# Layer 1's projections from one product of weights, q and k parts stored one by one, and four scatters or gathers under way

## The reference

```python
# layer 0
h = layernorm(x) * (1 + ca) + sa
q, k, v = split(h @ w_qkv.T)                # 16 heads of 8
x = x + ga * (softmax(q k' * SCALE) v @ w_out.T + b_out)
h = layernorm(x) * (1 + cb) + sb
comb = the two largest of softmax(h @ gate_w.T), of 8 experts, elsewhere 0
x = x + gb * (sum over e of comb[:, e] * swiglu_e(h) + swiglu_shared(h))   # hidden 352 and 192
# layer 1
q, k, v = h @ wq_lat @ wq_heads, h @ wk_lat @ wk_heads, h @ wv_lat @ wv_heads   # latents of 32
x = x + ga * (softmax(causal(q k' * SCALE)) v @ w_proj + b_proj)
x = x + gb * sum over e of comb[:, e] * (relu(h @ W1[e])**2 @ W2[e])            # 8 experts of 128
ga, gb = (2 * (g >= 0) - 1) * max(|g|, 0.25)     # in both layers
```

## Time and profile before

| | |
|---|---|
| Time, three runs | 1190.44, 1190.77, 1201.79 us; median 1190.77 |
| The profiled execution | 1188.06 us, its span 1185.7 us |
| PE busy | 1053.7 us, 89% of the span |
| DVE, ACT, POOL busy | 891.5, 743.6, 410.2 us |
| Mean granted clock of PE | 0.948 of full speed |

### The profile page before, as it was taken

How to read it: one execution, slowest core, us unless ns; L and a number is a source line. 1 busy time by engine, 2 the same in 40 slices (tenths; PEclk the granted TensorE clock), 3 DMA queues, 4 the chain that set the end, 5 groups by cost and what they waited for, 6 DMA issues and landing times.

```text
span 1185.7 us, 22774 instructions
## 1 busy us (share of the span) xinstructions
PE 1053.7 (89%) x8372; PEld 539.5 (45%) x8372; DVE 891.5 (75%) x1809; ACT 743.6 (63%) x1235; POOL 410.2 (35%) x462
## 2 busy tenths in 40 slices
PE   4588988889899997899999998998998999999985
PEld 2121222215354454455556565656664344444454
DVE  5899888988788876796667876787666777778354
ACT  3157777677566665667665665456665676866853
POOL 2100222252123434532244424343125663333452
PEclk9569999989999999999999999998999799999998
DMA  3815253656738558448577485675733533521110
GB/s 104 188 32 128 75 135 109 185 157 170 208 96 264 185 158 225 137 132 231 169 203 223 144 255 164 179 222 160 190 116 107 113 109 83 140 62 34 57 38 18
DMA packets 114798, 169.21 MB, mean 143 GB/s; under 512 B 19248, under 2 KB 79024, under 8 KB 114688
## 3 DMA queue, kind: packets, MB, share of 16 engines
q1 hardware_dynamic: 109376, 156.49, 46.3%
q0 software_dynamic: 4736, 10.49, 3.1%
q10 hardware_dynamic: 576, 0.79, 0.2%
HBM read 109.07 MB, written 58.62 MB: 141 GB/s over the span
## 4 chain that ended last, share of the span: by engine, by line
PE 39%; DMA 21%; DVE 18%; issue 9%; ACT 6%; POOL 4%; SPq 1%; POOLq 0%; ACTq 0%; DVEq 0%
DMA gr<-d_y,pos 10%; DVE nm L873 9%; PE ps L698 9%; PE ps L681 4%; PE ps L660 4%; PE ps L759 4%; DMA d_h<-hx,pos 3%; PE ps L775 3%; PE ps L782 3%; PE ps L767 3%; ACT ES L1221 3%; DMA DR<-d_r 2%; DMA d_u<-US 2%; DMA d_m<-nmp 2%; ACT xn L1153 1%
## 5 line engine op out<-in xcount | busy, mean ns | idle before, releaser
L873 DVE TENSOR_REDUCE nm<-ps 128x2 f32<-128x1024 f32 (+3 forms) x512 | 508.3, 1016 | 89.7 <-PE ps L666 56.3
L1221 ACT ACTIVATE ES<-ps 128x1024 f32<-128x1024 f32 (+3 forms) x512 | 431.3, 863 | 178.5 <-PE ps L681 93.4
L698 PE MATMUL ps<-ES,VS 128*9 128x512 f32 (+3 forms) x2048 | 236.1, 539 | 0.8 <-DVE hdx L1057 0.5
L660 PE MATMUL ps<-KS,QS 48*128 48x512 bf16 (+3 forms) x1024 | 187.3, 365 | 39.7 <-DVE nm L873 28.8
L681 PE MATMUL ps<-QS,KS 51*128 51x512 bf16 (+3 forms) x1024 | 181.7, 354 | 24.5 <-DVE nm L873 12.9
L759 PE MATMUL ps<-hsT,wst 128*128 128x128 f32 x1104 | 152.5, 284 | 3.9 <-DVE nm L873 1.2
L759 PEld LDWEIGHTS ps<-hsT,wst 128*128 128x128 f32 x1104 | 135.6, 193 | 33.6 <-issue 29.5
L681 PEld LDWEIGHTS ps<-QS,KS 51*128 51x128 bf16 x1024 | 50.2, 94 | 190.4 <-issue 73.5
L660 PEld LDWEIGHTS ps<-KS,QS 48*128 48x128 bf16 x1024 | 50.5, 95 | 170.0 <-DVE nm L873 67.7
L1423 POOL TENSOR_TENSOR ya<-ya,yS 128x512 f32<-128x512 f32 x49 | 62.7, 1279 | 154.3 <-DVE yS L1117 154.2
L1403 POOL DMA_INDIRECT gr<-d_y,pos x64 | 66.7, 1042 | 108.4 <-DMA gr<-d_y,pos 65.8
(11 more groups left out here) (187 smaller groups left out, 1341.2 us busy)
## 6 DMA issues: line engine op xcount, KB each, us to landing
wst<-we SPq DMA_DIRECT2D x92, 576.0 KB, 5.0
d_u<-US SPq DMA_DIRECT2D x64, 256.0 KB
KS<-d_k SPq DMA_DIRECT2D x64, 192.0 KB, 5.3
...
d_q<-sp SPq DMA_DIRECT2D x16, 384.0 KB, 2.8
d_k<-sp SPq DMA_DIRECT2D x16, 384.0 KB, 2.6
...
```

The lines of the kernel that those rows point to most:

```text
L660: mm = eng.matmul(psum[:, bank[u][a], 0:n], QS[m][r:r + KA, pr, 128 * t:128 * t + 128], KS[m][r:r + KA, pr, 0:n], start=True, stop=i < NB)
L698: mm = eng.matmul(psum[32 * a:32 * a + 9, b, q0:S], VS[i % 3][:, j, 4 * g + a, :], ES[(2 * (NT * (NG * i + g) + j) + a // 2) % NES][:, a % ...
L873: eng.tensor_reduce(nm[f][:, :].rearrange("p (a c) -> p a c", a=2)[:, :, 4 * pr + t], ps2("score", i, f, pr, t)[:, :, 0:n], AX.X, ALU.max, ...
L1221: eng.activation(ES[(2 * n + pp) % NES][:, :, 0:S - q0], ps2("bscore", i, f, g, j, pp)[:, :, 0:S - q0], ACT.Exp, scale=SC1 if i >= NB else ...
```

## The change

1. **Latents.** `p_lat` and `p_latc` go. Once, PE multiplies the latents by the head weights (`w_mm`, 384 columns), ACT copies the product over the head weights (`w_cp`), and in layer 1 q, k and v come from hP directly. The host lays the latents out transposed; the product is made on the chip.
2. **Parts of q and k.** Each part is a step of its own on SP and is issued when that part is ready. sr has two buffers, one for q and one for k. The four loads of a stack go KS, QS, KS, QS with the halves taken crosswise.
3. **Ones.** One memset makes rows of ones in a weight buffer not yet used (`c_one`, 32x1024), and eight DMAs carry three rows each into KS. `bscore` waits for them all, and so does the first use of that weight buffer.
4. **Scatters and gathers.** Each waits for the one four before it, not two; the scatters' semaphores are regrouped to four.
5. **Gates.** `m_fin` has five operations in place of nine, on two of three column groups at a time.
6. **The planner's numbers** are set anew, which moves steps on all engines.

The diff, cut to its core:

```diff
-SHIFT = {"t": -0.12, "s": 1.02, ... "d": 1.41, "x": 1.14, ... "g": -0.96, ...}
+SHIFT = {"t": -0.11, "s": 1.11, ... "d": 1.34, "x": 1.09, ... "g": -0.9, ...}
...
-    MOVES = {"stack": 2.7, "p_store": 3.4, ...
+    MOVES = {"stack": 3.8, "p_store": 0.8, ...
...
-SPREAD = 2.6, 1.8
+SPREAD = 2.4, 2.1
...
+        add("DVE", ("c_one",), 1.2, -1.0, [("m_one", 0)])
     for m in range(NSTK):
-        add("DVE", ("c_ks", m), 2.3, -1.0 + 0.3 * m, [("p_sub", 0, 1) if m else ("p_stats", 0)])
+        add("SP", ("c_ks", m), 0.8, 0.1 + 0.1 * m, [("c_one",)], lag=2.5)
...
+    add("PE", ("w_mm",), 0.75, 6.5, [("ld", "w1")], opens=1)
+    add("ACT", ("w_cp",), 0.4, 6.5, [("w_mm",)], closes=[("w_mm",)])
...
-                    add("DVE", ("g_w", i0, t), 0.58, u, [two, last, ("g_x", i0 - 1), ("m_st", 1)])
+                    add("DVE", ("g_w", i0, t), 0.75, u, sent[-2:] + [("g_x", i0 - 1), ("m_st", 1)])
...
-                elif k == "p_lat":
-                    i = u[1]
+                elif k == "w_mm":
+
                     q.wait_ge(*on("ld", "w1"))
-                    q.wait_ge(*on("p_ht", i))
-                    open_banks(u)
-                    eng.matmul(ps(*u), w1s[:, W1["lat"]:W1["lat"] + 128], hP, start=True, stop=True).then_inc(s[k], 1)
+                    open_banks(u)
+                    eng.matmul(ps(*u)[:, 0:384], w1s[:, W1["lat"]:W1["lat"] + 128], w1s[:, W1["q"]:W1["q"] + 384],
+                               start=True, stop=True).then_inc(s[k], 1)
...
-                elif k == "p_latc":
-                    i = u[1]
-                    q.wait_ge(*on("p_lat", i))
...
-                    eng.activation(lat, ps("p_lat", i), ACT.Copy).then_inc(s[k], 1)
+                elif k == "w_cp":
+                    q.wait_ge(*on("w_mm"))
+                    eng.activation(w1s[:, W1["q"]:W1["q"] + 384], ps("w_mm")[:, 0:384], ACT.Copy).then_inc(s[k], 1)
...
-                    if n:
-                        q.wait_ge(s["g_ga", 2 * ((n - 1) % 4) + c], 16 * ((n - 1) // 4 + 1))
+                    if n >= 2:
+                        q.wait_ge(s["g_ga", 2 * ((n - 2) % 4) + c], 16 * ((n - 2) // 4 + 1))
...
+                elif k == "c_ks":
+                    q.wait_ge(*on("c_one"))
+                    for a in range(2):
+                        eng.dma_start(KS[u[1]][64 * a + KA:64 * a + KB, :, :].rearrange("k h t -> k (h t)"),
+                                      ones[0:KB - KA, :].bitcast(BF16)).then_inc(s["ld", k], 16)
                 elif k == "p_store":
-                    i, n = u[1:]
-                    q.wait_ge(*on("p_hi", i, n))
-                    q.wait_ge(*on("p_mid", i, n))
-                    q.wait_ge(*on("p_lo", i, n))
-                    to = (d_q, d_k)[n][i]
-                    for c, (r, step, reps) in enumerate(PLACES[n]):
-                        eng.dma_start(bass.AP(tensor=to.tensor, offset=to.offset + r * 128 * S, ap=[[S, 128], [step * 128 * S, reps], [1, S]]),
-                                      sp[n][:, c:c + 1, :].broadcast_to([128, reps, S])).then_inc(s["p_store", n], 16)
+                    i, n, c = u[1:]
+                    q.wait_ge(*on(("p_hi", "p_mid", "p_lo")[c], i, n))
+                    to, (r, step, reps) = (d_q, d_k)[n][i], PLACES[n][c]
+                    eng.dma_start(bass.AP(tensor=to.tensor, offset=to.offset + r * 128 * S, ap=[[S, 128], [step * 128 * S, reps], [1, S]]),
+                                  sp[n][:, c:c + 1, :].broadcast_to([128, reps, S])).then_inc(s["p_store", n], 16)
...
-                    for a in range(2):
-                        for to, of in ((KS, d_k[i]), (QS, d_q[i])):
+                    for h in range(2):
+                        for a, to, of in ((h, KS, d_k[i]), (1 - h, QS, d_q[i])):
```

More of the change, by code:

```diff
@@ L243, in plan @@
         for n in range(2):
             u = i + 0.05 + 0.05 * n
-            add("PE", ("p_proj", i, n), 0.95, u, [x, ("ld", f"w{l}"), ("p_store", i - 1, n), ("p_sub", i - 1 + n, 1 - n)], opens=1)
-            add("ACT", ("p_hi", i, n), 0.49, u, [("p_proj", i, n), ("p_store", i - 1, n)])
-            add("DVE", ("p_sub", i, n), 0.6, u, [("p_hi", i, n), ("p_lo", i - 1 + n, 1 - n)], closes=[("p_proj", i, n)])
+            add("PE", ("p_proj", i, n), 0.95, u, [x] + ready, opens=1)
+            add("ACT", ("p_hi", i, n), 0.49, u, [("p_proj", i, n)] + [("p_store", i - 1, n, c) for c in range(3)])
@@ L254, in plan @@
             add("SP", ("stack", i, f), 2.1, i + 0.2 + 0.1 * f,
-                [("p_store", i, 0), ("p_store", i, 1), ("c_ks", (2 * i + f) % NSTK), ("bscore", i - 2, f, 1, NT - 1, 1)], lag=3.4)
+                [("p_store", i, n, c) for n in range(2) for c in range(3)] + [("bscore", i - 2, f, 1, NT - 1, 1)], lag=3.4)
         for f in range(2):
@@ L285, in plan @@
                     add("PE", ("bscore", i, f, g % 2, j, pp), 0.01 + 0.22 * n / 512 + 0.06 * (not big), u + 0.03 * pp,
-                        [("max_ld", i, f)] + exps[-2:-1] + old, mode="half", opens=2)
+                        [("max_ld", i, f)] + [("c_ks", m) for m in range(NSTK) if i == 0] + exps[-2:-1] + old, mode="half", opens=2)
                     add("ACT", ("expo", i, f, g % 2, j, pp), 0.06 + 2 * n * 0.00083, u + 0.03 * pp,
@@ L355, in plan @@
                         n = min(4, NMT - j)
-                        add("SP", ("x_ld", q, L), 0.45, u - 0.2, [two, last]
+                        add("SP", ("x_ld", q, L), 0.45, u - 0.2, sent[-4:]
                             + [("x_turn", q, L - 2) if L > 1 else ("x_turn", q - 1, NXL - 2 + L)], lag=3.1)
@@ L385, in plan @@
                     for k in range(2):
-                        add("POOL", ("g_ga", i0, t, k), 1.28, u, [("x_st", q, L) for L in range(NXL)] + [two, ("g_w",) + n2], lag=2.1)
-                        two, last = last, ("g_ga", i0, t, k)
-                    add("DVE", ("g_w", i0, t), 0.58, u, [two, last, ("g_x", i0 - 1), ("m_st", 1)])
+                        add("POOL", ("g_ga", i0, t, k), 1.28, u, [("x_st", q, L) for L in range(NXL)] + [sent[-4], ("g_w",) + n2], lag=2.1)
+                        sent.append(("g_ga", i0, t, k))
+                    add("DVE", ("g_w", i0, t), 0.75, u, sent[-2:] + [("g_x", i0 - 1), ("m_st", 1)])
                 add("POOL", ("g_x", i0), 2.6, u, [("g_w", i0, NT - 1), ("g_gc", i0), ("s_x", i0)])
@@ L543, in program @@
         for k in total:
-            if k not in DMAS and k not in ("ld", "p_store", "r_sc", "g_ga", "d_out", "c_h", "c_code"):
+            if k not in DMAS and k not in ("ld", "p_store", "r_sc", "g_ga", "d_out", "c_h", "c_code", "c_ks"):
                 s[k] = ctx.enter_context(nc.semaphore(k))
@@ L552, in program @@
             s["p_store", n] = ctx.enter_context(nc.semaphore(f"p_store{n}"))
-            for c in range(2):
-                s["r_sc", n, c] = ctx.enter_context(nc.semaphore(f"r_sc{n}{c}"))
         for name in ("t_mul", "r_hm", "rstd_a"):
@@ L557, in program @@
         rstd_a = {u: 2 * n + 1 for n, u in enumerate(u for u in todo["POOL"] if u[0] in ("p_rstd", "f_rstd"))}
+        for n in range(4):
+            s["r_sc", n] = ctx.enter_context(nc.semaphore(f"r_sc{n}"))
         for n in range(8):
@@ L1160, in _ @@
                     q.wait_ge(*on("m_one", l))
[L1161 removed]
+                    if w == 0 and i:
                         q.wait_ge(*on("p_v", i - 1))
@@ L1362, in _ @@
                         p = i // 2 - 1
-                        for c in range(2):
-                            q.wait_ge(s["r_sc", p % 2, c], 128 * (p // 2 + 1))
+                        for m in range(4):
+                            q.wait_ge(s["r_sc", m], 64 * (p + 1))
                     eng.tensor_tensor(hx[i % 2][:, :, :], xn[1][:, :, :], g[:, 2:3, :].broadcast_to([128, NT, 128]),
```

130 lines of the change are left out of this document (59 added, 71 removed).

## The result

| | |
|---|---|
| The changed kernel, four runs | 1214.12 to 1223.94 us, median 1220.55 |
| The kernel before, beside it | 1189.44 to 1201.79 us, median 1190.61 |
| Ratio | 1.0227, 95% interval 1.0163 to 1.0291: slower, by 1.6 to 2.9% |
| Forecast | 1174, range 1156 to 1192: the time lies outside, on the other side |

What follows compares the result with a forecast made beforehand. PE was taken as the bound, with DVE's row maxima setting the pace from 34 to 75 us. From 1188.06 us, -1.5 - 1.0 - 7.1 - 7.0 = -16.6 gave 1171.5, or 1174 for the median; range 1156 to 1192.

Steps and rivals of the forecast that it cites:

- The start: Loads and stores before the first score: earlier issue wins 1.5 us, between -4.8 and +2.7.
- The gates: DVE's nine operations from 75.52 to 78.53 us become five: -1 us, between 0 and -3.
- The latents: Sixteen PE records, 8.8 us, go and one product comes: -7.1 us, between 0 and -8.0.
- The gathers: DVE's combines in four pairs: four under way quicken gathers, stalls shrink to 3.2 us a pair, -7 us.
- the 1.8: The pace forecast for gathers with four under way: one each 1.8 us, beside 3.5 before.
- the moved steps: Steps that the planner's new numbers move on all engines: 0, with 5 us either way.
- The term of the scatters: Scatters ahead of the experts' tiles, where PE is at 96%: 0, to -4 us.
- The slower one: Rival: DVE comes to the combines too early and stalls longer: 1204 to 1247 us, chance 0.11.
- Gains turned into waiting: Rival: PE's saved time goes into waits for row maxima, gathers stall as before: 1188 us, chance 0.18.

Runs made afterwards that it cites:

- a4gap: The changed kernel, lists and waits of four kept, with POOL clearing 192 columns of a spare tile behind each scatter and gather: 1200.9 us, ratio 1.0085.
- p4: The changed kernel with lists written anew for two transfers under way, but waits of four: 1168.2 us, ratio 0.9817 to the kernel before.
- a2p: The changed kernel without its fourth part, lists written anew for two transfers under way and waits of two: 1179.5 us, ratio 0.9886 to the kernel before.

## Why the prediction was wrong, point by point

**The sum, as measured.** On some 1191 us: the parts without the fourth -13.6 (0.9886), waits of four on good lists -8 (to 0.9817, not clear of the noise), the lists written for four +49 (1.0227 against 0.9817; with waits of two as much). That is +27, the ratio found, as it must be, since each is a difference of two ratios. Of the 49 a gap of 512 columns takes back 20 (1.0227 to 1.0057), and 29 stay. That the stack behind the scatters makes most of what the lists cost is shown with waits of two, 33 of 48. With waits of four I read the 20 as the late signals and the 29 as the stack; this split is argued, not shown, as a4gap won 17 of the 20 with the signals late, and the two losses cover each other. What POOL's clearing of 512 columns costs by itself is within the 29, and was not measured apart.

**The start: right.** Timeline of the kernel after, beside the earlier trace rows:

```profile
7.02 2.73 PE L620 MATMUL ps<-cs,hd 128*128 128x8 f32 x12 [7.02 <-DVE cs L811]
...
10.41 0.91 DVE L803 MEMSET wst<- 32x1024 f32 x1
...
12.72 3.75 PE L645 MATMUL ps<-hP,w0s 128*128 128x512 f32 x4 [1.02 <-ACT hP L1174]
...
23.88 0.41 SPq L1482 DMA_DIRECT2D KS<-d_k  x1
...
31.56 1.03 PE L663 MATMUL ps<-KS,QS 48*128 48x512 bf16 x4 [6.61 <-DMA QS<-d_q]
```

The first product is at 7.02 and not 9.51, the first score at 31.56 and not 33.90: 2.3 us; I took 1.5. That 2.3 is also the sum at the issue is luck: the stack goes out 3.6 us earlier (23.88 for 27.46), more than the 2.3, and its landing takes 1.2 us more. In the other runs with these parts the stack goes out at 23.9 to 24.3 as well, and the first score comes between 30.8 and 33.5: the landing takes back a changing share.

**The gates: right.** Five operations, 1.5 us instead of 3.0:

```profile
74.28 0.40 DVE L830 SCALAR_TENSOR_TENSOR hx<-hx 8x256 f32<-8x256 f32 x1
...
75.58 0.21 DVE L839 TENSOR_SCALAR hx<-hx 8x128 f32<-8x128 f32 x1
```

**The latents: right in kind.** One product of 0.9 us stands for the 8.8:

```profile
L636 PE MATMUL ps<-w1s 128*128 128x384 f32 x2 | 0.9, 538 | 0.0
```

PE's busy time shows it only where the clock is as before: p4, at a mean granted clock of 0.947, is busy 1048.1 us, 5.6 less than before. These three came to 9.6 in the forecast and 13.6 in a2p; the order written anew is in that too, and I can't split it.

**The gathers: the pace was right, the gain came only on lists for two.** DVE's waits for them fell to 5.4 us (the forecast had 3.2 a pair, 12.8, beside 22.2 that left out 1.8 at L1074), and the combines of the first pair, 49.2 us from first to last before, took 33.6:

```profile
434.30 0.35 DVE L1076 SCALAR_TENSOR_TENSOR cv<-gr,wts,cv 128x128 f32<-128x128 f32 x1 [0.18 <-issue]
...
467.87 0.35 DVE L1076 SCALAR_TENSOR_TENSOR cv<-gr,wts,cv 128x128 f32<-128x128 f32 x1
```

That is 2.4 us a gather by the forecast's own measure; POOL issued them at 1.64 to 2.07 us each on the mean of a pair, as the 1.8 had it, and DVE was held by other waits, late signals among them. On lists for two DVE's waits for gathers fell from 24.5 us (a2p) to 6.1 (p4), and the 7 us forecast are near the 8 that the waits of four gave there, scatters included and not clear of the noise. But the change told the planner too, and so done, with scatters at two, the gathers cost 16 us (0.9886 to 1.0017) where -7 was forecast: the term asked how long DVE waits for a gather, and not what a run of them does to the other engines.

**The step that failed: the fourth part, above all scatters, "I take 0, to -4", and the moved steps, "0, with 5 either way".** The lists written for four cost 49 us in their place. The term of the scatters asked only what PE could win where it is at 96%, and never what an unbroken run does. The same edit, told to the planner, turned POOL's list into 16 scatters in one piece in three of four pairs (the longest of before are 12 and 14, and those go out under waits of two), with k's last part behind them. I had followed the moved steps on SP's and DVE's lists and not on POOL's, where this stood to be read. With scatters for four alone, lists and waits, the kernel lost 31 us (0.9886 to 1.0148). The late signals no row of before showed; the stack behind the scatters could have been worked out from the pace of 1.3 us and the order.

**The rivals.** None was it. The slower one looked at DVE, which should come too early to the combines: its waits for gathers fell to 5.4 us, so it is out, though it had the sign. "Gains turned into waiting" is out too: the other parts' gain is there in a2p. The Trainium skill, page "DMA: Bandwidth & Descriptors", section "Issuing engines are not separate DMA queues", says that transfers run on the same 16 DMA engines and interleave, whoever starts them; from that the prediction took it that more under way need not mean more moved. This is not what cost the time: in the third window above the 16 engines' share was 0.22. No run here shows the page wrong, but the section doesn't speak of what the run did to PE's signals.
